# Selective scan on one core: two more products with B on GpSimd, a B tile with an odd offset, and a copied column order in the dt stage

## The chip, the cores and the metric

The kernel runs on one core of a Trainium2 chip. The metric is the device time of one execution in microseconds (us), median of three runs. The engines are named as the profile names them: PE (TensorE matmul) and PEld (its weight loads), DVE (VectorE), ACT (ScalarE), POOL (GpSimd) and SPq (the DMA queue that SyncE feeds).

## The reference, cut to what matters

Layer 0 is a shifted-window attention block on 16 images of 56 x 56 tokens with 192 channels. Layer 1 is a selective scan in four directions (row order, column order, and both reversed) with 16 states for each channel:

```python
xs = _cross_scan(xc)                       # row order, column order, both reversed
x_dbl = jnp.einsum('bkdl,kcd->bkcl', xs, x_proj_weight)
dts, Bs, Cs = jnp.split(x_dbl, [R_RANK, R_RANK + N_STATE], axis=2)
dts = jnp.einsum('bkrl,kdr->bkdl', dts, dt_projs_weight)
dts = jax.nn.softplus(dts + dt_projs_bias[None, :, :, None])
...
dA = jnp.exp(dt_t[..., None] * A)
dBx = (dt_t * x_t)[..., None] * B_t[:, :, None, :]
h = dA * h_prev + dBx
y = jnp.einsum('bkdn,bkn->bkd', h, C_t)
```

## The kernel before

The program has four stages, one after the other: layer 0, the dt stage (`build_prep`), the scan (`build_scan`) and the output. Between stages the data lies in HBM. Each engine has its own written-out order of work and waits on counters (semaphores) of the others. The change touches the two middle stages.

**The dt stage** makes dt, u = dt * x, B and C. It works image by image, in four chunks (`PAIRS`) of 784 positions, and in each chunk on six tiles (`TILES`) of 128 rows: tiles 0 to 2 are the row order (o = 0), tiles 3 to 5 the column order (o = 1). A seventh piece of TensorE's work gives B and C. The columns of an image are read in column order by a view of the tile `xm` whose inner step is one image row, 56 words (224 bytes); that is what `order` returns for o = 1. For each tile TensorE computes the raw value into PSUM (L750 to L754, L759 and L762 for B and C), ACT copies it to `xb` (L780, a ring of four), clamps (L793), takes exp (L801) and log (L809, into PSUM). DVE then does four operations per tile: P, the `scalar_tensor_tensor` of `m_t` and the log (L858), then `quad` of the next tile (L848, whose two inputs are both `e_t` in SBUF), then a minimum (L863) and a maximum that gives dt (L867). The other three operations have one operand in PSUM. POOL multiplies dt by x (L884, `times_x`) and splits B and C into three bf16 parts, one operation in each of the places j = 1 to 4 of a chunk (`split`: L894 cast, L898 subtract, L901 cast, L904 subtract). SP stores dt, u, B and C, and loads the next image.

**The scan** has 256 units (16 images, 16 units each: order, chunk, direction), and a unit has 24 steps of 784 positions: three groups of eight state pairs. In a step ACT computes dA (L1133), DVE or POOL the product of u and B, and DVE the scan itself (L1199). In 17 steps DVE multiplies u by a B that TensorE spread into PSUM (L1054, L1176, `DVE_STEPS`), two steps ahead of the scan (`LEAD`). In the other 7 (`POOL_STEPS`, steps 3, 7, 11, 13, 15, 19, 23) POOL multiplies u by a B tile `bp_u` that a DMA loaded for state pairs 3, 5 and 7 (L1224), into the two-buffer ring `dbp`; it does so seven steps ahead. POOL also multiplies each two steps' states by C (L1235, 12 operations of 1568 columns in a unit), into a ring `pr` that TensorE sums (L1065). DVE's scan of a step waits until POOL has done the product with C of the step six earlier (`RH` = 6 buffers of `hs`):

```python
after(dve, prod_done, n - RH + 1)
```

The tiles `hs`, `dbx` and `dbp` are 786 columns wide with their data in columns 1 to 784 (`data`), so their data begins 4 bytes into a row whose start is a multiple of 8 bytes; `u_u`, `c_u`, `pr` and `bp_u` are 784 wide and begin at column 0. SP loads a unit's tiles when POOL has finished the unit two earlier, so they are used one unit later.

Of the kernel before, what the change touches and what calls it, by code (L numbers as in the profile page):

```python
# [556 lines left out]
POOL_STEPS = (3, 7, 11, 13, 15, 19, 23)  # L557
# [20 lines left out]
def build_prep(nc, io, xn, dts, us, bcs, bps, n_img):  # L578
# [7 lines left out]
    with ExitStack() as ctx:  # L586
# [20 lines left out]
        rem = sb("rem", [128, CT])  # L607
        parts = sb("parts", [128, 2, 3, CT], BF16)
# [6 lines left out]
        u_done = sem("u_done")  # L615
# [8 lines left out]
        def order(tile, o, c, h, n):  # L624

            t0 = CT * c + HT * h
            if o == 0:
                return tile[:, t0:t0 + n]
            return tile.rearrange("p (r w) -> p w r", r=IMG)[:, t0 // IMG:(t0 + n) // IMG, :]
# [92 lines left out]
        @block.tensor  # L722
        def _(pe):
            pe.wait_ge(w_in, 80)
            for k in range(4):
                pe.matmul(ps[:, k, 0:C], xpr_sb[:, k, 0:128], dtw_sb[:, k, :], start=True, stop=True)
            for k in range(4):
                pe.matmul(ps[0:64, k, 512:512 + C], xpr_sb[:, k, 128:C], dtw_sb[:, k, :], start=True, stop=True)
            for k in range(4):
                mm = pe.matmul(ps[64:128, k, 512:512 + C], xpr_sb[:, k, 128:C], dtw_sb[:, k, :], start=True, stop=True)  # L730
            mm.then_inc(w_mm, 1)
            pe.wait_ge(w_done, 1)

            def free(b, k):

                img, j = (0, k - 2) if k >= 2 else (-1, k - 2 + PER_IMG)
                if j % PER < TILES:
                    after(pe, xb_done, TILES * (PAIRS * (b + img) + j // PER) + j % PER + 1)
                else:
                    after(pe, bc_done, PAIRS * (b + img) + j // PER + 1)  # L740

            def body(b, par, last):
                pe.wait_ge(x_in[par], images_in(b, par))
                for k in range(PER_IMG):
                    c, j = k // PER, k % PER
                    free(b, k)
                    if j < TILES:
                        o, m0 = j // 3, 128 * (j % 3)
                        for h in range(2):
                            pe.matmul(bank(k, h), wk[:, o, 0, m0:m0 + 128], order(xm[:, par, 0, :], o, c, h, HT),  # L750
                                      start=True, stop=False)
                        pe.matmul(bank(k, 0), wk[0:64, o, 1, m0:m0 + 128], order(xm[0:64, par, 1, :], o, c, 0, HT),
                                  start=False, stop=True)
                        pe.matmul(bank(k, 1), wk[64:128, o, 2, m0:m0 + 128], order(xm[64:128, par, 2, :], o, c, 1, HT),  # L754
                                  start=False, stop=True).then_inc(raw_full, 1)
                    else:
                        for h in range(2):
                            for o in range(2):
                                pe.matmul(bank(k, h)[64 * o:64 * o + 64, :], wk[:, o, 0, 2 * C:KC],  # L759
                                          order(xm[:, par, 0, :], o, c, h, HT), start=True, stop=False)  # L760
                            for o in range(2):
                                mm = pe.matmul(bank(k, h)[64 * o:64 * o + 64, :], wk[0:64, o, 1, 2 * C:KC],  # L762
                                               order(xm[0:64, par, 1, :], o, c, h, HT), start=False, stop=True)
                        mm.then_inc(raw_full, 1)

            halves(pe, body)
# [62 lines left out]
        def _(dve):  # L829
# [20 lines left out]
            def body(b, par, last):  # L850
                for c in range(PAIRS):
                    g = PAIRS * b + c
                    for j in range(TILES):
                        n, o = TILES * g + j, j // 3
                        l = l_ps(j)
                        dve.wait_ge(l_done, n + 1)
                        dve.wait_ge(m_done, n + 1)
                        nc.vector.scalar_tensor_tensor(l, m_t[:, j % 2], -0.5, l, ALU.mult, ALU.max).then_inc(p_done, 1)  # L858
                        at = step(b, n_of(c, j) + 1, last)
                        if at:  # L860
                            quad(*at)
# [11 lines left out]
        def _(pool):  # L873

            def times_x(b, par, c, j):
# [5 lines left out]
                u = u_o[:, o, k, :]  # L881
                if o:
                    dt, u = (a.rearrange("p (w r) -> p w r", r=IMG) for a in (dt, u))
                nc.gpsimd.tensor_tensor(u, dt, order(xm[:, par, k, :], o, c, 0, CT), ALU.mult).then_inc(u_done, 1)  # L884
# [21 lines left out]
            def body(b, par, last):  # L906
                pool.wait_ge(x_in[par], images_in(b, par))
                for c in range(PAIRS):
                    for j in range(TILES):
# [4 lines left out]
                        elif not (isinstance(b, int) and b == 0):  # L914
                            times_x(b - 1, 1 - par, PAIRS - 1, TILES - 1)
                        if j in (1, 2, 3, 4):
# [8 lines left out]

            halves(pool, body)


def build_scan(nc, io, dts, us, bcs, bps, ysc, n_img):
# [9 lines left out]
    with ExitStack() as ctx:  # L939
# [18 lines left out]
        bp_u = sb("bp_u", [128, 2, len(POOL_PAIRS), CT])  # L958
# [26 lines left out]
        def _(sp):  # L985
# [5 lines left out]
            def load(b, w):  # L991
# [9 lines left out]
                for h in range(2):  # L1001
                    sp.dma_start(bp_u[64 * h:64 * h + 64, d],
# [211 lines left out]
        def _(pool):  # L1214

            def times_b(b, w, i):
# [4 lines left out]
                if not (isinstance(v, int) and v == 0 and i < RG):  # L1221
# [3 lines left out]
                                        bp_u[:, d, POOL_PAIRS.index(s % NPR), :], ALU.mult).then_inc(bp_done, 1)  # L1225

            def body(b, first, last):
                for w in range(WI):
                    v, d = WI * b + w, w % 2
                    pool.wait_ge(u_in[d], in_of(b, w))  # L1230
                    for s in range(0, STEPS, 2):
# [7 lines left out]
                        elif s + 7 - STEPS == POOL_STEPS[0]:  # L1239
                            if w + 1 < WI:  # L1240
                                times_b(b, w + 1, 0)
                            elif not last:
                                times_b(b + 1, 0, 0)

            times_b(0, 0, 0)
            images(pool, body, n_img)
# [302 lines left out]
```

## Time and profile before

| | us |
|---|---|
| median of three runs | 21221.99 (21221.65 to 21222.45) |
| the profiled execution | 21220.53 |
| its span | 21218.7 |
| dt stage, window taken | 4383 to 6290 |
| scan, window taken | 6334 to 20540 |
| DVE busy in the span | 18936.0 |
| POOL busy in the span | 15154.9 |
| TensorE's mean granted clock | 0.788 |

Busy times are those of one profiled execution. A start-to-start distance of two instructions in the timeline is a little shorter than a duration, because the end of one overlaps the start of the next. A granted clock of 1.00 is TensorE's level of 2.4 GHz, 0.50 that of 1.2 GHz.

### The profile page before, as it was taken

Reading aid. Unit: us, or ns where it says so; the run is one execution under the profiler, and the core shown is the slowest. Engines: PE = TensorE matmul, PEld = TensorE weight load, DVE = VectorE, ACT = ScalarE, POOL = GpSimd, SP = SyncE. Lnnn points to the kernel's source line nnn. Section 1 sums busy time; section 2 is a strip of 40 time slices with the busy share of each in tenths; the row PEclk is TensorE's granted clock in tenths of the full one; section 3 lists DMA queues with packets and bytes.
Section 4 is the critical chain, followed back from the end, with each engine's and each line's share of the span. In section 5 each row is a group of like instructions: output and inputs, shape, how many; then the busy total and the mean of one; then the engine's idle time right before and its main releaser. Section 6 shows DMA issues by size and latency. Waiting matters only on the chain. (4 is left out here: it accounts for less than half of the span.)

```text
span 21218.7 us, 290175 instructions
## 1 busy us (share of the span) xinstructions
PE 16258.9 (77%) x83096; PEld 5510.0 (26%) x83096; DVE 18936.0 (89%) x21113; ACT 10243.6 (48%) x19687; POOL 15154.9 (71%) x5780
## 2 busy tenths in 40 slices
PE   8999999999987777777777777777777777777752
PEld 5555555532221111111111111111111111111112
DVE  5555555579989999999999999999999999999986
ACT  4444444467764444444444444444444444444443
POOL 0000000046669999999999999999999999999988
PEclk9999999988987777777777777777777777777765
DMA  0000000056665666666666666666666666666668
GB/s 22 18 18 18 18 18 17 18 174 230 226 214 122 135 126 134 129 131 131 127 135 129 135 127 131 131 131 133 126 135 127 135 129 130 131 128 135 128 142 230
DMA packets 1091858, 2520.55 MB, mean 119 GB/s; under 512 B 247606, under 2 KB 398648, under 8 KB 1075328
## 3 DMA queue, kind: packets, MB, share of 16 engines
q1 hardware_dynamic: 1090688, 2508.11, 52.6%
q14 instruction: 822, 6.73, 0.1%
q8 instruction: 348, 5.70, 0.1%
HBM read 2000.43 MB, written 507.38 MB: 118 GB/s over the span
## 5 line engine op out<-in xcount | busy, mean ns | idle before, releaser
L1235 POOL TENSOR_TENSOR c_pr<-c_hs,c_c_u 128x1568 f32<-128x1568 f32 x3072 | 9929.8, 3236 | 1040.9 <-DVE c_hs L1199 761.9
L1133 ACT ACTIVATE c_psum<-c_dt_u,c_a_neg 128x784 f32<-128x784 f32 x6144 | 5641.8, 918 | 7476.7 <-DVE c_hs L1199 7419.7
L1199 DVE TENSOR_TENSOR_SCAN c_hs<-c_psum,c_dbx 128x785 f32<-128x785 f32 (+1 forms) x4352 | 7606.2, 1770 | 20.9 <-issue 20.9
L1065 PE MATMUL c_psum<-c_pr,c_red 128*64 128x392 f32 x24576 | 7222.4, 707 | 1.3 <-POOL c_pr L1235 1.3
L1054 PE MATMUL c_psum<-c_br_u,c_sel 48*128 48x512 bf16 (+1 forms) x8704 | 2966.6, 433 | 4024.7 <-DVE c_dbx L1176 3925.3
L1176 DVE TENSOR_TENSOR c_dbx<-c_u_u,c_psum 128x784 f32<-128x784 f32 x4352 | 4086.9, 939 | 39.6 <-PE c_psum L1054 39.6
L1224 POOL TENSOR_TENSOR c_dbp<-c_u_u,c_bp_u 128x784 f32<-128x784 f32 x1792 | 3312.4, 1848 | 105.9 <-DVE c_hs L1199 63.7
L1199 DVE TENSOR_TENSOR_SCAN c_hs<-c_psum,c_dbp 128x785 f32<-128x785 f32 (+1 forms) x1792 | 3186.0, 1778 | 0.0
L196 POOL TENSOR_TENSOR a_xpb<-a_x_sb,a_pb_sb 98x768 f32<-98x768 f32 x128 | 231.1, 1806 | 4062.5 <-DVE a_x L285 4048.9
L1065 PEld LDWEIGHTS c_psum<-c_pr,c_red 128*64 128x64 f32 x24576 | 1790.2, 177 | 3403.3 <-issue 3120.7
L1054 PEld LDWEIGHTS c_psum<-c_br_u,c_sel 48*128 48x128 bf16 x8704 | 522.4, 101 | 8208.9 <-DVE c_dbx L1176 7004.6
L884 POOL TENSOR_TENSOR p_u_o<-p_dt_o,p_xm 128x784 f32<-128x784 f32 x384 | 786.7, 2049 | 715.2 <-DVE p_dt_o L867 715.2
L750 PE MATMUL p_psum<-p_xm,p_wk 128*128 128x392 f32 x1536 | 910.2, 722 | 81.9 <-ACT p_xb L780 70.6
L848 DVE SCALAR_TENSOR_TENSOR p_m_t<-p_e_t 128x784 f32<-128x784 f32 x384 | 777.7, 2025 | 15.2 <-ACT p_e_t L801 15.2
L235 DVE TENSOR_REDUCE a_mx<-a_psum 128x6 f32<-128x294 f32 x512 | 234.2, 457 | 617.2 <-PE a_psum L461 617.2
L329 ACT ACTIVATE a_g_sb<-a_psum,a_b_sb 128x392 f32<-128x392 f32 x768 | 408.6, 583 | 519.1 <-PE a_psum L426 519.1
L424 PE MATMUL a_psum<-a_h2T,a_w_sb 128*128 128x392 f32 x1536 | 609.1, 519 | 60.2 <-ACT a_h2T L312 60.2
L436 PE MATMUL a_psum<-a_g_sb,a_w_sb 128*128 128x392 f32 x1536 | 607.8, 518 | 53.6 <-ACT a_g_sb L329 53.6
L285 DVE TENSOR_TENSOR a_x<-a_xpb,a_psum 98x384 f32<-98x384 f32 x256 | 142.0, 555 | 525.1 <-PE a_psum L536 525.1
L1115 ACT ACTIVATE c_dbx<-c_carry 128x1 f32<-128x1 f32 x3264 | 608.5, 186 | 0.0
L780 ACT ACTIVATE p_xb<-p_psum,p_bpos 128x784 f32<-128x784 f32 x384 | 349.6, 910 | 439.9 <-DVE p_dt_o L867 411.0
L1471 PE MATMUL d_psum<-d_id_sb,d_yf 96*112 96x96 f32 x896 | 155.2, 361 | 510.1 <-POOL d_yf L1350 390.9
(119 smaller groups left out, 17276.6 us busy)
## 6 DMA issues: line engine op xcount, KB each, us to landing
c_c_u<-scr_bc SPq DMA_DIRECT2D x512, 1568.0 KB, 28.7
c_dt_u<-scr_dt SPq DMA_DIRECT2D x512, 588.0 KB, 7.3
c_u_u<-scr_u SPq DMA_DIRECT2D x512, 588.0 KB, 10.9
c_bp_u<-scr_bc SPq DMA_DIRECT2D x512, 588.0 KB, 22.1
scr_dt<-p_dt_o SPq DMA_DIRECT2D x384, 392.0 KB, 3.1
scr_u<-p_u_o SPq DMA_DIRECT2D x384, 392.0 KB, 2.4
scr_y<-c_y_sb SPq DMA_DIRECT2D x256, 294.0 KB, 17.7
d_yin<-scr_y SPq DMA_DIRECT2D x32, 2352.0 KB, 14.5
```

Source lines behind the costliest of these rows:

```text
L424: pe.matmul(ps[:, gate(m + f), 0:UT], w1_sb[:, 0, w(f)], h2T[:, 0, :], start=True, stop=False)
L750: pe.matmul(bank(k, h), wk[:, o, 0, m0:m0 + 128], order(xm[:, par, 0, :], o, c, h, HT), start=True, stop=False)
L848: nc.vector.scalar_tensor_tensor(m_t[:, j % 2], e, -2.0, e, ALU.add, ALU.mult).then_inc(m_done, 1)
L884: nc.gpsimd.tensor_tensor(u, dt, order(xm[:, par, k, :], o, c, 0, CT), ALU.mult).then_inc(u_done, 1)
L1054: mm = pe.matmul(b_ps[:, n0:n1], sel[:, s % NPR, :], br_u[:, d, n0:n1], start=True, stop=True)
L1065: mm = pe.matmul(Y(3 * w + q)[64 * h:64 * h + 64, :], red[:], pr[:, s % RP, HT * h:HT * h + HT], start=(p == 0 and opens(w)), stop=(p == N ...
L1115: nc.scalar.activation(end, carry[:, d, s:s + 1], ACT.Copy)
L1133: nc.scalar.activation(dA(s)[:, data], dt_u[:, d, s // NPR, :], ACT.Exp, scale=a_neg[:, k, s:s + 1]).then_inc(exp_done, 1)
L1176: nc.vector.tensor_tensor(dbx[:, (MULS * w + i) % RB, data], u_u[:, d, s // NPR, :], b_ps, ALU.mult).then_inc(mul_done, 1)
L1199: nc.vector.tensor_tensor_scan(hs[:, s % RH, way], dA(s)[:, way], added, 0.0, ALU.mult, ALU.add).then_inc(scan_done, 1)
L1224: nc.gpsimd.tensor_tensor(dbp[:, (len(POOL_STEPS) * w + i) % RG, data], u_u[:, d, s // NPR, :], bp_u[:, d, POOL_PAIRS.index(s % NPR), :], ...
L1235: nc.gpsimd.tensor_tensor(pr[:, s % RP:s % RP + 2, :], hs[:, s % RH:s % RH + 2, data], c_u[:, d, s % NPR:s % NPR + 2, :], ALU.mult).then_i ...
```

## The change

In the scan POOL takes steps 5 and 21 as well: nine products with B instead of seven, DVE fifteen instead of seventeen. The tile `bp_u` becomes 786 columns wide, with its data in columns 1 to 784. POOL's product for the second place of the next unit is now issued at the end of a unit too.

In the dt stage POOL copies the column-order view of a chunk to a new tile `xt`, contiguous, one chunk ahead (`turn`, three copies in a chunk in the places j = 0, 1 and 3, behind `times_x` and ahead of `split`). TensorE's matmuls and POOL's `times_x` of the column order read `xt`. Ahead of the first column-order tile of a chunk TensorE waits for the chunk's copies. On DVE `quad` of the next tile stands ahead of P instead of behind it.

```diff
-POOL_STEPS = (3, 7, 11, 13, 15, 19, 23)
+POOL_STEPS = (3, 5, 7, 11, 13, 15, 19, 21, 23)
...
+        xt = sb("xt", [128, 2, 3, CT])
...
-        def order(tile, o, c, h, n):
-
-            t0 = CT * c + HT * h
+        def order(rows, par, k, o, c, h, n):
+
             if o == 0:
-                return tile[:, t0:t0 + n]
-            return tile.rearrange("p (r w) -> p w r", r=IMG)[:, t0 // IMG:(t0 + n) // IMG, :]
+                return xm[rows, par, k, CT * c + HT * h:CT * c + HT * h + n]
+            return xt[rows, c % 2, k, HT * h:HT * h + n]
...
+                    if j == TILES // 2:
+                        pe.wait_ge(turned, 3 * (PAIRS * b + c) + 3)
...
+                        at = step(b, n_of(c, j) + 1, last)
+                        if at:
+                            quad(*at)
                         dve.wait_ge(l_done, n + 1)
                         dve.wait_ge(m_done, n + 1)
                         nc.vector.scalar_tensor_tensor(l, m_t[:, j % 2], -0.5, l, ALU.mult, ALU.max).then_inc(p_done, 1)
-                        at = step(b, n_of(c, j) + 1, last)
-                        if at:
-                            quad(*at)
...
-                u = u_o[:, o, k, :]
-                if o:
-                    dt, u = (a.rearrange("p (w r) -> p w r", r=IMG) for a in (dt, u))
-                nc.gpsimd.tensor_tensor(u, dt, order(xm[:, par, k, :], o, c, 0, CT), ALU.mult).then_inc(u_done, 1)
+                nc.gpsimd.tensor_tensor(u_o[:, o, k, :], dt, order(slice(0, 128), par, k, o, c, 0, CT),
+                                        ALU.mult).then_inc(u_done, 1)
+
+            def turn(b, par, c, k):
+
+                g = PAIRS * b + c
+                if k == 0:
+                    if c == 0:
+                        hold(pool, x_in[par], images_in(b, par), fence)
+                    if not (isinstance(g, int) and g < 2):
+                        hold(pool, u_done, TILES * (g - 1), fence)
+                        hold(pool, raw_full, PER * (g - 1), fence)
+                cols = xm[:, par, k, :].rearrange("p (r w) -> p w r", r=IMG)[:, CT * c // IMG:CT * (c + 1) // IMG, :]
+                nc.gpsimd.tensor_copy(xt[:, c % 2, k, :].rearrange("p (w r) -> p w r", r=IMG), cols).then_inc(turned, 1)
...
+                        if j in (0, 1, 3):
+                            if c + 1 < PAIRS:
+                                turn(b, par, c + 1, (0, 1, 3).index(j))
+                            elif not last:
+                                turn(b + 1, 1 - par, 0, (0, 1, 3).index(j))
...
+            for k in range(3):
+                turn(0, 0, 0, k)
...
-        bp_u = sb("bp_u", [128, 2, len(POOL_PAIRS), CT])
+        bp_u = sb("bp_u", [128, 2, len(POOL_PAIRS), CT + 2])
...
-                    sp.dma_start(bp_u[64 * h:64 * h + 64, d],
+                    sp.dma_start(bp_u[64 * h:64 * h + 64, d, :, data],
...
-                                        bp_u[:, d, POOL_PAIRS.index(s % NPR), :], ALU.mult).then_inc(bp_done, 1)
+                                        bp_u[:, d, POOL_PAIRS.index(s % NPR), data], ALU.mult).then_inc(bp_done, 1)
...
-                        elif s + 7 - STEPS == POOL_STEPS[0]:
+                        elif s + 7 - STEPS in POOL_STEPS:
+                            i = POOL_STEPS.index(s + 7 - STEPS)
                             if w + 1 < WI:
-                                times_b(b, w + 1, 0)
+                                times_b(b, w + 1, i)
                             elif not last:
-                                times_b(b + 1, 0, 0)
+                                times_b(b + 1, 0, i)
 
             times_b(0, 0, 0)
+            times_b(0, 0, 1)
```

## Rows read from the trace of the kernel before

**Rows 1.** By window: us, busy (PE, PEld, DVE, ACT, POOL), clock, DMA.

```profile
4383.00:6290.00 1907.00, 1786.31 (x4090) 471.70 (x4088) 1806.79 (x1536) 1359.43 (x1600) 1280.47 (x639) 0.90 0.66 223
6334.00:20540.00 14206.00, 10241.70 (x34048) 2462.22 (x34048) 14175.67 (x10496) 6720.68 (x13568) 13097.21 (x4864) 0.72 0.63 130
```

**Rows 2.** The page's costliest groups, those of the scan.

```profile
L1235 POOL TENSOR_TENSOR c_pr<-c_hs,c_c_u 128x1568 f32<-128x1568 f32 x3072 | 9929.8, 3236 | 1040.9 <-DVE c_hs L1199 761.9
...
L1199 DVE TENSOR_TENSOR_SCAN c_hs<-c_psum,c_dbx 128x785 f32<-128x785 f32 (+1 forms) x4352 | 7606.2, 1770 | 20.9 <-issue 20.9
...
L1176 DVE TENSOR_TENSOR c_dbx<-c_u_u,c_psum 128x784 f32<-128x784 f32 x4352 | 4086.9, 939 | 39.6 <-PE c_psum L1054 39.6
L1224 POOL TENSOR_TENSOR c_dbp<-c_u_u,c_bp_u 128x784 f32<-128x784 f32 x1792 | 3312.4, 1848 | 105.9 <-DVE c_hs L1199 63.7
```

**Rows 3.** Timeline of VectorE in the scan: start, us, operation.

```profile
12004.18 1.78 DVE L1199 TENSOR_TENSOR_SCAN c_hs<-c_psum,c_dbx 128x785 f32<-128x785 f32 x1
...
12006.75 3.46 DVE L1199 TENSOR_TENSOR_SCAN c_hs<-c_psum,c_dbx 128x785 f32<-128x785 f32 x2
12010.13 0.94 DVE L1176 TENSOR_TENSOR c_dbx<-c_u_u,c_psum 128x784 f32<-128x784 f32 x1
```

**Rows 4.** Timeline of GpSimd in the scan.

```profile
12022.23 1.84 POOL L1224 TENSOR_TENSOR c_dbp<-c_u_u,c_bp_u 128x784 f32<-128x784 f32 x1 [0.24 <-DVE c_hs L1199]
12024.02 6.43 POOL L1235 TENSOR_TENSOR c_pr<-c_hs,c_c_u 128x1568 f32<-128x1568 f32 x2
12030.41 1.84 POOL L1224 TENSOR_TENSOR c_dbp<-c_u_u,c_bp_u 128x784 f32<-128x784 f32 x1
```

**Rows 5.** Timeline of the DMA queue in the scan.

```profile
12053.77 1.38 SPq L997 DMA_DIRECT2D c_dt_u<-scr_dt  x2
...
12060.15 0.74 SPq L1004 DMA_DIRECT2D c_c_u<-scr_bc  x1
...
12109.14 1.38 SPq L997 DMA_DIRECT2D c_dt_u<-scr_dt  x2
```

**Rows 6.** Landing of the last load: DMA issues, KB each, us to landing.

```profile
c_c_u<-scr_bc SPq DMA_DIRECT2D x512, 1568.0 KB, 28.7
```

**Rows 7.** GpSimd's groups by shape, whole span.

```profile
L1350 POOL TENSOR_TENSOR d_yf<-d_yin 96x3136 f32<-96x3136 f32 x32 | 267.3, 8355 | 39.5 <-DVE d_yin L1383 39.5
```

**Rows 8.** The dt stage by line: times run, shortest, median, longest in ns.

```profile
L884 POOL TENSOR_TENSOR p_u_o<-p_dt_o,p_xm x384: 1840/2048/2272, 4394.7 to 6284.8; 128x784 f32<-128x784 f32 x192
...
L894 POOL CAST p_parts<-p_bc_o x64: 836/1585/1600, 4431.6 to 6286.9; 128x784 bf16<-128x784 f32 x64
...
L898 POOL TENSOR_TENSOR p_rem<-p_bc_o,p_parts x64: 1665/2404/2426, 4436.3 to 6287.8; 128x784 f32<-128x784 f32 x64
...
L848 DVE SCALAR_TENSOR_TENSOR p_m_t<-p_e_t x384: 968/2056/2429, 4388.4 to 6277.5; 128x784 f32<-128x784 f32 x192
```

**Rows 9.** Timeline of the dt stage.

```profile
5200.97 0.97 DVE L863 TENSOR_TENSOR p_psum<-p_psum,p_e_t 128x784 f32<-128x784 f32 x1
5201.98 0.97 DVE L867 TENSOR_TENSOR p_dt_o<-p_xb,p_psum 128x784 f32<-128x784 f32 x1
...
5202.86 0.97 DVE L858 SCALAR_TENSOR_TENSOR p_psum<-p_m_t,p_psum 128x784 f32<-128x784 f32 x1
5203.03 1.85 POOL L884 TENSOR_TENSOR p_u_o<-p_dt_o,p_xm 128x784 f32<-128x784 f32 x1 [1.28 <-DVE p_dt_o L867]
...
5203.74 1.97 DVE L848 SCALAR_TENSOR_TENSOR p_m_t<-p_e_t 128x784 f32<-128x784 f32 x1
...
5204.84 2.40 POOL L898 TENSOR_TENSOR p_rem<-p_bc_o,p_parts 128x784 f32<-128x784 f32 x1
...
5205.56 1.58 PE L750 MATMUL p_psum<-p_xm,p_wk 128*128 128x392 f32 x4
...
5213.27 3.13 PE L750 MATMUL p_psum<-p_xm,p_wk 128*128 128x392 f32 x4 [0.52 <-ACT p_xb L780]
```

**Rows 10.** Busy time in one tile of the copied order, columns as in rows 1.

```profile
5213.20:5218.30 5.10, 4.75 (x8) 1.02 (x8) 5.07 (x5) 3.47 (x6) 4.67 (x3) 1.00 0.41 161
```

More of the change, by code:

```diff
@@ L614, in build_prep @@
         m_done, p_done, q_done, dt_done = sem("m_done"), sem("p_done"), sem("q_done"), sem("dt_done")
-        u_done = sem("u_done")
+        u_done, turned = sem("u_done"), sem("turned")
         hi_done, rem_done, mid_done, low_done = sem("hi_done"), sem("rem_done"), sem("mid_done"), sem("low_done")
@@ L749, in body @@
                         for h in range(2):
-                            pe.matmul(bank(k, h), wk[:, o, 0, m0:m0 + 128], order(xm[:, par, 0, :], o, c, h, HT),
+                            pe.matmul(bank(k, h), wk[:, o, 0, m0:m0 + 128], order(slice(0, 128), par, 0, o, c, h, HT),
                                       start=True, stop=False)
-                        pe.matmul(bank(k, 0), wk[0:64, o, 1, m0:m0 + 128], order(xm[0:64, par, 1, :], o, c, 0, HT),
+                        pe.matmul(bank(k, 0), wk[0:64, o, 1, m0:m0 + 128], order(slice(0, 64), par, 1, o, c, 0, HT),
                                   start=False, stop=True)
-                        pe.matmul(bank(k, 1), wk[64:128, o, 2, m0:m0 + 128], order(xm[64:128, par, 2, :], o, c, 1, HT),
+                        pe.matmul(bank(k, 1), wk[64:128, o, 2, m0:m0 + 128], order(slice(64, 128), par, 2, o, c, 1, HT),
                                   start=False, stop=True).then_inc(raw_full, 1)
@@ L759, in body @@
                                 pe.matmul(bank(k, h)[64 * o:64 * o + 64, :], wk[:, o, 0, 2 * C:KC],
-                                          order(xm[:, par, 0, :], o, c, h, HT), start=True, stop=False)
+                                          order(slice(0, 128), par, 0, o, c, h, HT), start=True, stop=False)
                             for o in range(2):
                                 mm = pe.matmul(bank(k, h)[64 * o:64 * o + 64, :], wk[0:64, o, 1, 2 * C:KC],
-                                               order(xm[0:64, par, 1, :], o, c, h, HT), start=False, stop=True)
+                                               order(slice(0, 64), par, 1, o, c, h, HT), start=False, stop=True)
                         mm.then_inc(raw_full, 1)
```

## The prediction

> **What bounds the kernel now.** I read the busy times by stage first. In the scan's window DVE is busy 14176 of 14206 us and POOL 13097; in the dt stage DVE 1807 of 1907 and PE 1786 [rows 1]. DVE sets the pace of the scan alone: a scan followed by a product takes 2.57 us (12004.18 to 12006.75), two scans without a product between them 3.38, so 1.69 each [rows 3]. Seventeen of the one and seven of the other give 17 x 2.57 + 7 x 1.69 = 55.5 us; from one unit's first load to the next unit's is 55.37 [rows 5]. POOL is close behind: two products with C take 6.39 us from start to start (3.195 each), a product with B 1.79 [rows 4], so a unit has 12 x 3.195 + 7 x 1.80 = 50.9 us of POOL's work and 4.4 us of rest.
>
> The dt stage spreads 384 tiles over 1890 us (first to last start of POOL's u product, 383 intervals, 4.94 us each), so 29.6 us for a chunk of six [rows 8]. The slow piece is `quad` (L848): it runs in 0.97 us at best and takes 2.06 in the median. The timeline shows what holds it: POOL's u product starts at 5203.03, `quad` at 5203.74, and `quad` ends at 5205.71, 0.87 us after POOL's next start at 5204.84 [rows 9]. The reverse holds too: that POOL subtract takes 2.40 us, 1.665 at best, and the cast 1.585, 0.836 at best [rows 8, 9]. So `quad` and a POOL operation exclude each other, and the one that waits gets in when the other ends, even if POOL has more queued. DVE's other three operations keep 0.97 beside POOL; only `quad` has two inputs in SBUF.
>
> **The scan's change.** Two products leave DVE. Each is worth 2.57 - 1.69 = 0.88 us, since a scan then follows a scan. 2 x 0.88 x 256 units = 450 us, and the unit becomes 55.37 - 1.76 = 53.61 us, if DVE still sets the pace.
>
> POOL gets nine products with B. At their present price it needs 12 x 3.195 + 9 x 1.80 = 54.54 us, more than DVE's 53.61, and POOL would be the bound. So all hangs on what the odd offset of `bp_u` does. Before shows no product with B in the new form. The nearest row is the product with C: 1568 columns in 3236 ns, 2.06 ns a column, against 1848 ns for 784, 2.36 [rows 2]. Part of this is a fixed cost. POOL's two operations with one strided input give it: 3136 columns in 8355 ns [rows 7] and 784 in some 2250 (the longest is 2272 [rows 8]), so 2.60 ns a column and 0.21 us fixed. With 0.21 fixed, the product with C runs at 1.93 ns a column and the one with B at 2.09. Only a fixed cost of 0.46 us would make them equal, and then the whole-tile cast would have 0.38 us for 784 columns, four times the rate of the product. What differs is the placing: C's product reads `hs` from an odd word and `c_u` from an even one; B's reads both from even ones, and the contiguous u product of the dt stage, both even too, takes 1840 ns at best [rows 8]. An odd output alone does not help, as B's has one. The padded tile gives B's product C's placing, so I take 0.21 + 784 x 1.93 ns = 1.725 us (0.12 less), 1.68 from start to start. POOL then needs 38.34 + 9 x 1.68 = 53.5 us, just under DVE's. The bounds: 1.62 with no fixed cost, 1.85 if the offset does nothing, 2.25, the strided row, if it harms.
>
> Can two engines this close run without stopping each other? I laid out eight steps by the code's waits. DVE's eight steps take 17.9 us, POOL's four products with C and three with B 17.8. POOL's product for step 7 stands behind the product with C of steps 0 and 1 but reuses the buffer of step 3's scan; POOL then starts some 1 us later than it could, keeps that lag, and meets no further wait. DVE needs that product with C only at step 6, 5 us later. So neither stops the other. The loads: the last is issued 6.4 us after the first [rows 5] and lands 28.7 us on [rows 6], 35 of a unit's 53; they are needed at step 20, at 45 us. The number and size of transfers do not change. If they were slower by the odd offset, ten us cover it. ACT waits on DVE's scan throughout (two scans in a row stand in rows 3 already) and is not reached.
>
> **The dt stage's change.** Three pieces.
>
> PE: a tile of the row order has its first four matmuls in 1.58 us, one of the column order in 3.13 [rows 9], at a granted clock of 1.00, so 2.4 GHz, in that very tile [rows 10]. It is the strided read, not the clock. Read from `xt` they are all fast. PE's chunk is 1786 / 64 = 27.9 us busy [rows 1], a third of it row order and two thirds column order; with the latter halved it is 18.6, no bound, and even at the scan's granted clock (0.72 [rows 1]) 18.6 / 0.72 = 25.8 us. POOL's u product of the column order falls from 2.25 to 1.85.
>
> DVE: its tile costs 0.88 between operations that don't depend on each other (max to P, P to `quad`), 1.01 between min and max that do [rows 9]. In the new order P to min also depends: 0.88 + 0.88 + 1.01 + 1.01 = 3.78 us if `quad` never waits. `quad` now follows the max directly and takes the port before the u product that waits for that max; POOL starts 0.9 us later, under DVE's three other operations. DVE then waits only for what POOL still has queued.
>
> POOL: three copies more in a chunk, each with one strided input. No such row exists. Below, the contiguous cast at its best, 0.84; above, the strided two-input product, 2.25. I take half of the contiguous product for its contiguous read, and the rest of the strided one for the strided: 2.25 - 0.85 = 1.4 us.
>
> A chunk laid out by hand, from the port's rule: after a max, `quad` holds the port 0.87, the u product 1.81, then the extras. Where a copy follows (three places) `quad` waits 0.87 + 1.81 + 1.4 - 3.78 = 0.3 us; where a subtract ends last (two places, behind a cast that came late) 0.87 + 0.80 + 1.81 + 1.62 - 3.78 = 1.3 us. Chunk: 6 x 3.78 + 3 x 0.3 + 2 x 1.3 = 26.2 us. Saved: (29.6 - 26.2) x 64 = 218 us. With a copy of 0.84 the chunk is some 24.7 (313 us saved), with 2.25 it is 28.8 (51 saved). The three copies ahead of the loop run under the first tiles of the row order.
>
> The Trainium skill's GPSIMD Engine Reference, section Performance pitfalls for Q7 kernels, prices reads with a step above 8 bytes at about 2.9 cycles an element. At 1.2 GHz that is an estimate of 1.9 us for a copy, a chunk of 27.7 and 122 us saved, 96 less than my sum; its contiguous 1.9 cycles are more than the cast shows here (0.836 us for 784, 1.3 cycles).
>
> **Sum.** 21220.5 of the profiled execution (1.5 us below the median) - 450 - 218 = 20553 us.
>
> **Rivals.**
> POOL becomes the bound of the scan. The offset does nothing, POOL needs 54.54 us, the scan saves (55.37 - 54.54) x 256 = 212 instead of 450: 21220.5 - 212 - 218 = 20790. For it: the product with C also differs by its length and its two-row shape, and the fixed cost is from operations of another form. Against: that fixed cost would have to be double.
> The same page, section Instruction dispatch, gives about 2.5 cycles an element as the floor of a two-input operation and says nothing of offsets; by it the price stays and this rival is the result. The row of the product with C (2.06 ns, 2.5 cycles) fits that floor, the one with B (2.8 cycles) leaves room above it.
>
> The port takes the dt stage's gain. If POOL's longer queue keeps `quad` out for more than one operation, DVE waits a copy and a cast or the u product as well and a chunk stays near 29.6: 21220.5 - 450 = 20770. Against it stands the subtract that let `quad` in [rows 9].
>
> Slower: the odd offset harms the second input. Priced as the strided row, 2.25 us (2.21 from start to start), a unit takes 38.34 + 9 x 2.21 = 58.2 us, 2.86 more than now, + 732 - 218: 21735. It decides from a product of 1.99 us start to start, since 9 x 1.99 + 38.34 = 56.2 eats the dt stage's 0.85 us a unit. Against: `hs` is read at an odd word at the better rate.
>
> **How the numbers follow.** Forecast 0.60, POOL as bound 0.27, the port 0.08, the slower one 0.04, nothing gained at all 0.01. A measurement of this kernel tells 0.2%, some 42 us, from no change. All but the last two are faster: faster 0.95, same 0.01, slower 0.04. The forecast's own range is 20450 (copies at 0.84) to 20720 (2.25). POOL as bound reaches from 20695 to 20957; I go up to 20840 and leave its tail and the slower case out.
>
> **What would show it.** Scan: L1224 at 1.72 us, DVE without idle, load to load 53.6 us. At 1.85 POOL has no idle, DVE waits for L1235 or L1224, and load to load is 54.5. dt stage: `quad` near 0.97 to 2.3 with waits behind L904 and L898; PE's four matmuls 1.58 us in all tiles; a new copy of 1.4 us; u product 1.85, shown longer where it waits for `quad`. The prediction fails most easily on B's product and on the copy.

## The result, and the profile after

The changed kernel takes 20603.72 us (median of four runs, 20602.78 to 20604.99) against 21222.22; the ratio is 0.9708, 95% interval 0.9692 to 0.9725. The forecast was 20553 us, 51 us too low; the range of 20450 to 20840 holds it.

Busy times of the dt stage and of the scan after the change, columns as in [rows 1]:

```profile
4383.00:6120.00 1737.00, 1338.75 (x4096) 482.57 (x4094) 1642.29 (x1540) 1359.57 (x1600) 1589.69 (x832) 0.86 0.72 245
6157.00:19925.00 13768.00, 9529.81 (x33024) 2403.81 (x33024) 13725.95 (x9984) 6717.75 (x13568) 13665.17 (x5376) 0.74 0.65 134
```

The first line answers to the dt stage's of before: the stage is shorter and PE's work in it fell from 1786 to 1339 us. The second is the scan: DVE is busy 13726 of 13768 us and POOL 13665, so both engines are now full.

The costliest groups of the scan, from the page:

```profile
L1254 POOL TENSOR_TENSOR c_pr<-c_hs,c_c_u 128x1568 f32<-128x1568 f32 x3072 | 9908.8, 3236 | 13.4 <-DVE c_hs L1218 12.9
...
L1218 DVE TENSOR_TENSOR_SCAN c_hs<-c_psum,c_dbx 128x785 f32<-128x785 f32 (+1 forms) x3840 | 6737.2, 1770 | 20.7 <-issue 20.7
...
L1218 DVE TENSOR_TENSOR_SCAN c_hs<-c_psum,c_dbp 128x785 f32<-128x785 f32 (+1 forms) x2304 | 4104.9, 1782 | 11.4 <-ACT c_psum L1152 11.4
L1243 POOL TENSOR_TENSOR c_dbp<-c_u_u,c_bp_u 128x784 f32<-128x784 f32 x2304 | 3943.0, 1711 | 127.8 <-DVE c_hs L1218 76.3
L1195 DVE TENSOR_TENSOR c_dbx<-c_u_u,c_psum 128x784 f32<-128x784 f32 x3840 | 3621.8, 943 | 39.9 <-PE c_psum L1073 39.9
```

They answer to [rows 2]. DVE does 3840 products instead of 4352, at nearly the same duration (943 ns, 939 before). POOL does 2304 products with B instead of 1792, at 1711 ns instead of 1848. POOL's rest ahead of the products with C fell from 1041 to 13 us.

From the first to the last scan the stage took 14193 us before and 13755 now, 55.44 and 53.73 us a unit: 438 us saved. From the first to the last u product the dt stage took 1890 us before and 1710 now, 29.6 and 26.8 us a chunk: 180 us saved. Together they are the 618 us of the result; the other stages kept their time.

The mean of 1711 ns hides what matters. The timeline of GpSimd in the scan:

```profile
12036.79 3.24 POOL L1254 TENSOR_TENSOR c_pr<-c_hs,c_c_u 128x1568 f32<-128x1568 f32 x1
12039.99 1.58 POOL L1243 TENSOR_TENSOR c_dbp<-c_u_u,c_bp_u 128x784 f32<-128x784 f32 x1
12041.52 3.24 POOL L1254 TENSOR_TENSOR c_pr<-c_hs,c_c_u 128x1568 f32<-128x1568 f32 x1
12044.72 1.85 POOL L1243 TENSOR_TENSOR c_dbp<-c_u_u,c_bp_u 128x784 f32<-128x784 f32 x1
12046.52 6.42 POOL L1254 TENSOR_TENSOR c_pr<-c_hs,c_c_u 128x1568 f32<-128x1568 f32 x2
```

The product with B takes 1.58 us or 1.85 us, nothing between. Going through all 2304 in order, and naming them by the tile row that they read (six rows: two directions times three pairs), each row has one duration (median of 384 products each):

| row of `bp_u` (a word is 4 bytes) | 0 | 1 | 2 | 3 | 4 | 5 |
|---|---|---|---|---|---|---|
| begins, in words modulo four | 1 | 3 | 1 | 3 | 1 | 3 |
| us | 1.575 | 1.850 | 1.573 | 1.846 | 1.575 | 1.840 |

Every tile starts at a multiple of four words in these kernels, so the places can be counted from the tile's start. A row is 786 words, two more than a multiple of four, so the rows alternate. Half of the products gained 0.27 us, half gained nothing.

In the dt stage, lines with times run and shortest, median and longest in ns:

```profile
L883 POOL TENSOR_TENSOR p_u_o<-p_dt_o,p_xm x192: 1835/2582/2615, 4397.4 to 6096.9; 128x784 f32<-128x784 f32 x192
...
L896 POOL COPY p_xt<-p_xm x192: 1621/1644/1697, 4382.4 to 6074.7; 128x784 f32<-128x784 f32 x192
...
L850 DVE SCALAR_TENSOR_TENSOR p_m_t<-p_e_t x384: 968/1328/2165, 4391.7 to 6100.6; 128x784 f32<-128x784 f32 x192
...
L752 PE MATMUL p_psum<-p_xt,p_wk x768: 492/493/1023, 4391.2 to 6088.3; 128*128 128x392 f32 x192
```

And of the timeline, the first four matmuls of a column-order tile:

```profile
5165.57 1.58 PE L752 MATMUL p_psum<-p_xt,p_wk 128*128 128x392 f32 x4
```

`quad` (L850) has a median of 1.33 us instead of the 2.06 of [rows 8]. The u product (L883) is shown at 2.58, since it now starts behind `quad` and its wait for the port is in its span; 1.84 is its own time. A copy takes 1.64 us. Four of TensorE's matmuls of the column order in a row now take 1.58 us, as those of the row order did; before they took 3.13 [rows 9].

The same stage in order of time:

```profile
5178.45 1.64 POOL L896 COPY p_xt<-p_xm 128x784 f32<-128x784 f32 x1
5178.73 0.97 DVE L869 TENSOR_TENSOR p_dt_o<-p_xb,p_psum 128x784 f32<-128x784 f32 x1
...
5179.62 1.32 DVE L850 SCALAR_TENSOR_TENSOR p_m_t<-p_e_t 128x784 f32<-128x784 f32 x1
...
5180.05 1.58 POOL L906 CAST p_parts<-p_bc_o 128x784 bf16<-128x784 f32 x1
...
5180.86 0.97 DVE L863 SCALAR_TENSOR_TENSOR p_psum<-p_m_t,p_psum 128x784 f32<-128x784 f32 x1
```

The copy (L896) starts at 5178.45, and DVE's maximum (L869) runs beside it at its usual 0.97. `quad` starts at 5179.62 and ends at 5180.94, 0.85 us after the copy's end (5180.09); the cast behind the copy, 0.83 us at its best, then takes 1.58. This is the exclusion of [rows 9], with a copy as the one that goes first: `quad` loses 0.35 us here, where it lost 1.0 in [rows 9]. It holds throughout: 307 of the 384 `quad`s take over 1.05 us while a POOL operation ends inside them, and each of these ends 0.83 to 0.85 us after that operation's end.

### The profile page after: what moved, and what is told of

It reads as the page before. It is cut to its first block and busy times, and to the rows that moved or that the text cites. A ratio compares the mean times of both kernels' runs of the same rounds, so it can differ in the third digit from the quotient of the medians.

```text
span 20602.3 us, 287674 instructions
## 1 busy us (share of the span) xinstructions
PE 15096.4 (73%) x82072; PEld 5460.7 (27%) x82072; DVE 18321.8 (89%) x20601; ACT 10241.1 (50%) x19687; POOL 16030.5 (78%) x6484
## 5 line engine op out<-in xcount | busy, mean ns | idle before, releaser
L1254 POOL TENSOR_TENSOR c_pr<-c_hs,c_c_u 128x1568 f32<-128x1568 f32 x3072 | 9908.8, 3236 | 13.4 <-DVE c_hs L1218 12.9
L1084 PE MATMUL c_psum<-c_pr,c_red 128*64 128x392 f32 x24576 | 6829.8, 679 | 5.9 <-POOL c_pr L1254 5.9
L1218 DVE TENSOR_TENSOR_SCAN c_hs<-c_psum,c_dbx 128x785 f32<-128x785 f32 (+1 forms) x3840 | 6737.2, 1770 | 20.7 <-issue 20.7
L1073 PE MATMUL c_psum<-c_br_u,c_sel 48*128 48x512 bf16 (+1 forms) x7680 | 2596.8, 430 | 4293.5 <-DVE c_dbx L1195 4191.0
L1218 DVE TENSOR_TENSOR_SCAN c_hs<-c_psum,c_dbp 128x785 f32<-128x785 f32 (+1 forms) x2304 | 4104.9, 1782 | 11.4 <-ACT c_psum L1152 11.4
L1243 POOL TENSOR_TENSOR c_dbp<-c_u_u,c_bp_u 128x784 f32<-128x784 f32 x2304 | 3943.0, 1711 | 127.8 <-DVE c_hs L1218 76.3
L1195 DVE TENSOR_TENSOR c_dbx<-c_u_u,c_psum 128x784 f32<-128x784 f32 x3840 | 3621.8, 943 | 39.9 <-PE c_psum L1073 39.9
L850 DVE SCALAR_TENSOR_TENSOR p_m_t<-p_e_t 128x784 f32<-128x784 f32 x384 | 579.4, 1509 | 46.3 <-ACT p_e_t L803 26.7
L752 PE MATMUL p_psum<-p_xt,p_wk 128*128 128x392 f32 x768 | 364.1, 604 | 270.7 <-ACT p_xb L782 270.2
L1134 ACT ACTIVATE c_dbx<-c_carry 128x1 f32<-128x1 f32 x2880 | 537.0, 186 | 0.0
L883 POOL TENSOR_TENSOR p_u_o<-p_dt_o,p_xt 128x784 f32<-128x784 f32 x192 | 442.7, 2306 | 85.1 <-DVE p_dt_o L869 83.7
```

Of the source, the lines that this page charges most:

```text
L850: nc.vector.scalar_tensor_tensor(m_t[:, j % 2], e, -2.0, e, ALU.add, ALU.mult).then_inc(m_done, 1)
L883: nc.gpsimd.tensor_tensor(u_o[:, o, k, :], dt, order(slice(0, 128), par, k, o, c, 0, CT), ALU.mult).then_inc(u_done, 1)
L1073: mm = pe.matmul(b_ps[:, n0:n1], sel[:, s % NPR, :], br_u[:, d, n0:n1], start=True, stop=True)
L1084: mm = pe.matmul(Y(3 * w + q)[64 * h:64 * h + 64, :], red[:], pr[:, s % RP, HT * h:HT * h + HT], start=(p == 0 and opens(w)), stop=(p == N ...
L1134: nc.scalar.activation(end, carry[:, d, s:s + 1], ACT.Copy)
L1195: nc.vector.tensor_tensor(dbx[:, (MULS * w + i) % RB, data], u_u[:, d, s // NPR, :], b_ps, ALU.mult).then_inc(mul_done, 1)
```

## The experiments

### Nine products from an unpadded tile

```diff
-        bp_u = sb("bp_u", [128, 2, len(POOL_PAIRS), CT + 2])
+        bp_u = sb("bp_u", [128, 2, len(POOL_PAIRS), CT])
```

The load and the product use columns 0 to 783 accordingly.

> The changed kernel, with the B tile 784 columns wide again, data from the first column. In the changed kernel the product with B shows two durations: 1.57 us for rows 0, 2 and 4 of the tile (of six, two directions times three pairs) and 1.85 us for rows 1, 3 and 5; the tile is 786 words wide, so even rows begin 1 word and odd rows 3 words behind a multiple of four words. Theory (the placing of the second input sets the rate): all nine products take 1.85 us, GpSimd needs 12 x 3.195 + 9 x 1.80 = 54.54 us a unit against 53.73 now, and becomes the bound: 20604 + 0.81 x 256 = 20811 us. Rival (the two durations come from what else runs at that moment, not from the tile's place): two durations stay, time 20604.

Measured: 20826.29 us, ratio to before 0.9813 (0.9797 to 0.9829). The product with B over the whole run, and the scan's window:

```profile
L1243 POOL TENSOR_TENSOR c_dbp<-c_u_u,c_bp_u x2304: 1825/1855/2007, 6156.8 to 20134.6; 128x784 f32<-128x784 f32 x192
```

```profile
6157.00:20140.00 13983.00, 9539.74 (x33002) 2395.61 (x33002) 13763.85 (x9984) 6715.86 (x13567) 13964.59 (x5375) 0.74 0.64 132
```

All six rows have medians of 1.85 to 1.86 us, POOL is busy 13965 of 13983 us and DVE only 13764. A unit is 54.59 us, where the sum of POOL's operations gave 54.54. This is the prediction's first rival, made to happen: without the offset POOL is the bound, and the offset is worth 223 us here.

### A probe of all places

```diff
-        bp_u = sb("bp_u", [128, 2, len(POOL_PAIRS), CT + 2])
+        bp_u = sb("bp_u", [128, 2, len(POOL_PAIRS), CT + 1])
...
-        hs = sb("hs", [128, RH, CT + 2])
+        hs = sb("hs", [128, RH, CT + 3])
```

The data of `bp_u` begins at column 0, so that its row r begins r words on.

> A probe in the changed kernel: the B tile is 785 words wide with data from the first column, so its six rows begin 0, 1, 2, 3, 4 and 5 words behind the start; the state tile hs is 787 wide, so its six rows begin 1, 0, 3, 2, 1, 0 words (modulo 4) behind a multiple of four. Theory (place modulo four words): the product with B takes 1.57 us at rows 1 and 5, 1.85 at 0, 3 and 4; row 2 is not known from what has run, 1.57 or 1.85. The product with C, two rows in one operation, took 3.235 with rows at 1 and 3, as one fast and one slow half would; now it must show at least two durations over its three row pairs (3.23 for a fast and a slow half, some 3.5 for two slow ones, some 2.95 for two fast ones). Rival (every second row is fast, whatever its place): B rows 0, 2 and 4 at 1.57 and C at 3.235 throughout. GpSimd gets slower in the mean: some 20700 to 20850 us.

Measured: 20804.41 us, one run. GpSimd's timeline:

```profile
12010.02 1.88 POOL L1243 TENSOR_TENSOR c_dbp<-c_u_u,c_bp_u 128x784 f32<-128x784 f32 x1
12011.82 3.54 POOL L1254 TENSOR_TENSOR c_pr<-c_hs,c_c_u 128x1568 f32<-128x1568 f32 x1
12015.29 1.89 POOL L1243 TENSOR_TENSOR c_dbp<-c_u_u,c_bp_u 128x784 f32<-128x784 f32 x1
12017.11 2.99 POOL L1254 TENSOR_TENSOR c_pr<-c_hs,c_c_u 128x1568 f32<-128x1568 f32 x1
12020.03 1.60 POOL L1243 TENSOR_TENSOR c_dbp<-c_u_u,c_bp_u 128x784 f32<-128x784 f32 x1
```

The product with C (L1254) now has two durations as well, 3.54 and 2.99 here. By rows, medians over the run:

| operation | first input begins at | second input at | second behind first, modulo four words | us |
|---|---|---|---|---|
| B, rows 0 and 4 | 0 | 0 | 0 | 1.85, 1.87 |
| B, rows 1 and 5 | 0 | 1 | 1 | 1.57 |
| B, row 2 | 0 | 2 | 2 | 1.58 |
| B, row 3 | 0 | 3 | 3 | 1.85 |
| C, `hs` rows 0 and 1, or 4 and 5 | 1 and 0 | 0 | 3 and 0 | 3.51 |
| C, `hs` rows 2 and 3 | 3 and 2 | 0 | 1 and 2 | 2.96 |

One rule fits all lines: fast when the second input begins 1 or 2 words behind the first, modulo four words, slow at 0 or 3. Offset 2 is even and fast, offset 3 is odd and slow, so "odd" was the wrong word. The rival, every second row whatever its place, is out: row 1 was slow before and is fast here. In all these products one of the two inputs begins at a multiple of four words; what happens when both begin off it was not tried, so "behind the first" is shown for these pairs alone.

### Wider rows, both ways round

Both kernels make `bp_u` and `hs` 788 words wide, so that all their rows begin alike. In the first `hs` begins one word behind a multiple of four, in the second three:

```diff
-        bp_u = sb("bp_u", [128, 2, len(POOL_PAIRS), CT + 2])
+        bp_u = sb("bp_u", [128, 2, len(POOL_PAIRS), CT + 4])
...
-        hs = sb("hs", [128, RH, CT + 2])
+        hs = sb("hs", [128, RH, CT + 4])
```

> The changed kernel with the B tile and the state tile hs 788 columns wide, data from the second column in both, so every row begins one word behind a multiple of four. From the probe: a two-input product on GpSimd is fast when its second input begins 1 or 2 words behind the first (modulo four words), slow at 0 or 3. Theory: the product with B (u at 0, B at 1) takes 1.57 us in all rows; the product with C (hs at 1, C at 0, so 3 behind) has two slow halves, 3.50. GpSimd needs 12 x 3.47 + 9 x 1.53 = 55.4 us a unit, and the time is 20604 + (55.4 - 53.73) x 256 = some 21030 us. Rival (an odd word in either input is enough): both fast, 2.96 for C, time 20604 or a little less.

Measured: 21087.46 us, ratio 0.9925 (0.9893 to 0.9956), over 400 us slower than the changed kernel. The profiled execution took 21045, with a unit of 55.44 us where the expectation had 55.4; why the other seven took some 40 us more is not known.

```profile
L1243 POOL TENSOR_TENSOR c_dbp<-c_u_u,c_bp_u x2304: 1561/1577/2005, 6155.3 to 20350.4; 128x784 f32<-128x784 f32 x192
...
L1254 POOL TENSOR_TENSOR c_pr<-c_hs,c_c_u x3072: 3475/3526/3963, 6163.5 to 20358.9; 128x1568 f32<-128x1568 f32 x192
```

The second kernel has this in place of the last line:

```diff
+        hs = sb("hs", [128, RH, CT + 4])[:, :, 2:CT + 4]
```

> As the run with rows of 788, but hs begins at the fourth column (3 words behind a multiple of four), so C is 1 word behind it. Theory: product with C 2.96, with B 1.57; GpSimd needs 12 x 2.92 + 9 x 1.53 = 48.8 us a unit and no longer matters; VectorE's 53.6 us set the time, 20604 less the 0.1 us a unit that VectorE now loses: 20575 to 20604 us. Rival (VectorE loses more to GpSimd than its idle time shows): clearly below 20570 us.

Measured: 20588.45 us, ratio 0.968 (0.9606 to 0.9753).

```profile
L1243 POOL TENSOR_TENSOR c_dbp<-c_u_u,c_bp_u x2304: 1562/1575/1617, 6155.4 to 19894.4; 128x784 f32<-128x784 f32 x192
...
L1254 POOL TENSOR_TENSOR c_pr<-c_hs,c_c_u x3072: 2949/2962/2980, 6163.7 to 19902.1; 128x1568 f32<-128x1568 f32 x192
```

Two kernels that differ by two columns' shift of one tile: the product with C takes 3.53 us in one and 2.96 in the other, with no overlap between the ranges. The rule holds whichever of the two inputs is the displaced one. Twice 1.575 less 2.962 leaves 0.19 us as the fixed cost of one operation, close to the 0.21 of the prediction.

In the second kernel POOL has time to spare; its waits show it (us in total, times, longest):

```profile
POOL c_dbp L1243 <- DVE c_hs L1218: 915.5, 766, 1.2
```

The changed kernel had 75 us there. A unit is 53.68 us, VectorE's own work, and 15 us of the time were gained: that is what the near tie cost the changed kernel. It did not cost it as a wait of VectorE for GpSimd; no such wait is in the changed kernel's list. These are:

```profile
ACT c_y_sb L1142 <- DMA scr_y<-c_y_sb: 74.9, 29, 3.8
...
DVE c_hs L1218 <- ACT c_psum L1152: 11.4, 17, 1.2
```

ScalarE waits for the store of y, and VectorE 11.4 us for ScalarE's exp behind it. With GpSimd faster the first wait is 42.4 us and the second is gone. In the code SyncE issues that store behind a unit's loads, which wait for GpSimd's products, so a late GpSimd makes the store late; this link is read from the code and not tested by itself. The wait for the store is taken away below, with eleven products.

### The dt stage alone, and its two halves

Only the dt stage's change, with the scan of before:

> Only the change of the dt stage; the scan is as before (seven products, B tile 784 wide). If the two parts add up: dt stage 177 us shorter as in the changed kernel, so 21222 - 177 = 21045 us, and the product with B at 1.85. Rival (the parts interact, since the scan's first loads or the order of buffers profit): differs from 21045 by over 40 us.

Measured: 21040.29 us, ratio 0.9914 (0.9898 to 0.9931); the chunk is 26.79 us, the unit 55.44. The parts add up within 5 us.

Only the order on DVE (`quad` ahead of P), in the kernel before:

> The kernel before, with quad ahead of P on VectorE and nothing else. Theory (TensorE's strided reads are the next bound): quad no longer waits for the u product, but TensorE needs 27.9 us of work for a chunk of 29.6, so the chunk falls to 28 us at best and the copies are needed for the rest: 21222 - (29.6 - 28.0) x 64 = 21120 us, and TensorE idles hardly at all. Rival (VectorE and the port alone set the pace): without the copies GpSimd has less on the port, the chunk is 22.7 + 2 x 1.3 + 0.4 for the longer u product = 25.7 us, and the time 20970 us.

Measured: 21123.04 us, ratio 0.9954 (0.9937 to 0.997). The dt stage, and `quad`:

```profile
4383.00:6191.00 1808.00, 1759.51 (x4088) 435.12 (x4087) 1489.58 (x1536) 1349.85 (x1600) 1301.05 (x639) 0.99 0.69 235
```

```profile
L848 DVE SCALAR_TENSOR_TENSOR p_m_t<-p_e_t x384: 966/968/2421, 4388.1 to 6178.7; 128x784 f32<-128x784 f32 x192
```

`quad` has a median of 0.97 us, most of its waits are gone, and yet the chunk is 28.07 us: PE is busy 1760 of 1808 us at a granted clock of 0.99, in effect the level of 2.4 GHz. The strided reads of the column order are the bound, as the first theory had it.

Only the copies, with `quad` behind P as before:

> The changed kernel with quad behind P again, so that of the dt stage's change only the copied column order is left. Theory (VectorE and the port are the bound, as the prediction has it): quad waits for the whole u product again, 4.66 us for a tile as the row-order tiles had, and a copy with a cast behind it delays the next u product by some 0.5 us in two places: a chunk of 28.0 + 0.6 = 28.6 us against 26.8, and 20604 + 1.8 x 64 = 20719 us. Rival (TensorE's faster reads alone were most of the gain): 20604 to 20640 us.

Measured: 20742.39 us, ratio 0.9774 (0.9758 to 0.979), the chunk 28.96 us.

```profile
L850 DVE SCALAR_TENSOR_TENSOR p_m_t<-p_e_t x384: 968/1968/2272, 4390.3 to 6238.0; 128x784 f32<-128x784 f32 x192
```

`quad` waits for the u product again, 1.97 in the median. Each half alone gives little, 1.5 us of a chunk for the order and 0.65 for the copies; together they give 2.8. Each takes away a bound that hides the other's gain.

### The copies on ScalarE

`turn` moves from POOL to ACT as `nc.scalar.activation(..., ACT.Copy)`, in the places j = 2, 3 and 4; POOL waits for `turned` ahead of the first column-order product.

> The changed kernel with the three copies of a chunk on ScalarE instead of GpSimd (places j = 2, 3 and 4 of a chunk). Theory (a copy costs by the wait for the port that it puts ahead of quad): quad's three waits behind the copies, 3 x 0.54 us, go; a chunk falls from 26.8 to 25.2 us, 20604 - 1.6 x 64 = 20500 us. Rival (ScalarE, with 21.2 us of work in a chunk and some 1 us for each copy, delays the exp and log that VectorE waits for): no gain or a loss, 20604 or more.

Measured: 20600.77 us, ratio 0.9708 (0.9692 to 0.9724), the same as the changed kernel. The dt stage; DVE's wait for the exp; the copies:

```profile
4383.00:6110.00 1727.00, 1326.95 (x4093) 470.67 (x4092) 1552.01 (x1540) 1632.90 (x1791) 1267.55 (x640) 0.87 0.73 246
```

```profile
DVE p_m_t L870 <- ACT p_e_t L803: 116.2, 105, 15.9
```

```profile
L823 ACT ACTIVATE p_xt<-p_xm x192: 1641/1665/1715, 4380.5 to 6063.3; 128x784 f32<-128x784 f32 x192
```

The rival was right. The port is relieved (DVE is busy 1552 instead of 1642 us), but a copy takes ACT 1.67 us, not 1, and ACT is busy 1633 of 1727 us; DVE waits 116 us for the exp, 27 in the changed kernel. In a chunk the waits inside `quad` fell by 1.5 us and those for the exp rose by 1.4. A copy takes nearly the same on both engines (1.64 and 1.67 us). Its length alone does not make it so: ACT's exp and clamp of 784 contiguous columns take 0.94 us in the same run.

### x one word off in the dt stage

```diff
-        xm = sb("xm", [128, 2, 3, L])
+        xm = sb("xm", [128, 2, 3, L + 4])[:, :, :, 1:L + 1]
...
-        xt = sb("xt", [128, 2, 3, CT])
+        xt = sb("xt", [128, 2, 3, CT + 4])[:, :, :, 1:CT + 1]
```

> The changed kernel, with x and its copied column order in the dt stage one word behind a multiple of four (both tiles four columns wider). Theory: the u product falls from 1.85 to 1.57 us, quad's waits by 0.28 us in five places of a chunk, 1.4 x 64 = 90 us: 20515 us. Rival 1 (waits are set by the subtracts and copies alone): 20604 us. Rival 2 (TensorE reads x at an odd word more slowly): the matmuls of the dt stage get longer and the gain is lost.

Measured: 20529.64 us, ratio 0.9652 (0.9579 to 0.9725), 74 us below the changed kernel; the chunk is 25.64 us.

```profile
L883 POOL TENSOR_TENSOR p_u_o<-p_dt_o,p_xm x192: 1563/2299/2330, 4396.7 to 6022.7; 128x784 f32<-128x784 f32 x192
...
L850 DVE SCALAR_TENSOR_TENSOR p_m_t<-p_e_t x384: 968/1060/2269, 4390.9 to 6026.4; 128x784 f32<-128x784 f32 x192
```

The u product is 1.56 us at its best instead of 1.84, and `quad` has a median of 1.06 us; its waits fell by 1.25 us a chunk, a little less than five times 0.28. The rule of the scan holds in another stage.

### Eleven products on GpSimd

With both products fast, POOL has room. `POOL_PAIRS` becomes (1, 3, 5, 7) and POOL takes all odd steps but step 1; DVE keeps thirteen.

> The kernel with the fast placings, and eleven products with B on GpSimd (all odd steps but step 1; the B tile holds four state pairs), thirteen on VectorE. Theory (work of the two engines is all that counts): VectorE 53.61 - 2 x 0.88 = 51.9 us a unit, GpSimd 12 x 2.92 + 11 x 1.53 = 51.9: 20604 - 1.8 x 256 = 20140 us at best. Rival (at a tie the two engines stop each other: a product with B two steps after the last reuses a ring buffer that is free only when the scan is there): some 0.5 to 1 us a unit more, 20270 to 20400 us.

Measured: 20285.21 us, ratio 0.9537 (0.9465 to 0.9609), a unit of 52.47 us where the work alone gives 51.9. The time lies in the range that the rival named, but not for the rival's reason. Waits of its scan:

```profile
ACT c_y_sb L1142 <- DMA scr_y<-c_y_sb: 216.3, 30, 8.0
...
DVE c_hs L1218 <- ACT c_psum L1152: 121.8, 26, 5.3
...
DVE c_hs L1218 <- POOL c_pr L1254: 17.8, 5, 3.6
```

POOL is not it: DVE waits 18 us for it. ACT waits 216 us for the store of y before it may write the y tile again, its exp stands behind that, and DVE waits 122 us for the exp. With x one word off as well:

> The kernel with the fast placings and eleven products with B on GpSimd, and with x one word off in the dt stage too. If the two gains add up: 20285 - 74 = 20211 us.

Measured: 20215.11 us, ratio 0.9525 (0.9509 to 0.9541). They add up. Then a fifth y tile, for the unit that opens an order right after the one that closed the same chunk:

```diff
-        y_sb = sb("y_sb", [128, NCHK, 3, HT])
+        y_sb = sb("y_sb", [128, NCHK + 1, 3, HT])
...
+        def place(o, cc):
+
+            return NCHK if o and cc == 0 else cc
```

> The kernel with eleven products and x one word off, and a fifth tile for the scan's results y, so that the unit that opens an order no longer writes the tile that the unit just before it closed. In the run with eleven products a unit took 52.47 us where 53.68 - 2 x 0.88 = 51.92 were expected; ScalarE waited 216 us for the transfer that stores y, and VectorE 122 us for ScalarE's next exp. Theory (that wait is the difference): a unit falls to some 51.95 us, the time to 20215 - 0.53 x 256 = 20080 us. Rival (the tie between VectorE and GpSimd costs the half microsecond, and would show as waits for GpSimd once ScalarE's is gone): 20180 to 20215 us.

Measured: 20070.0 us, ratio 0.9457 (0.9441 to 0.9472), a unit of 51.92 us. What is left of VectorE's and GpSimd's waits in the scan:

```profile
DVE c_hs L1222 <- issue: 21.4, 13, 2.1
POOL c_dbp L1247 <- DVE c_hs L1222: 13.5, 13, 1.1
```

No wait of ACT for the store and none of DVE for ACT or POOL remains in the list of waits. The unit is what DVE's work adds up to. This version beats both kernels: 1152 us below the kernel before, 534 below the changed one.

## Why the prediction was right, and where it was off

**What bounds the scan.** Right. Two products fewer are worth 0.88 us each: 55.44 less 1.76 is 53.68, the unit of the kernel with fast placings, and eleven products give 51.92. Forecast 450 us, measured 438. "Neither stops the other" held: VectorE has no listed wait for GpSimd. The 12 us missing are nearly all the 11.4 us that VectorE waited for ScalarE, behind the store of y; they came back (15 us) when POOL got faster.

**The product with B.** The size was right, 1.725 forecast and 1.711 measured, and with it the step on which all hung; in part this was luck. The mechanism was half right. The prediction reasoned that C's product is faster by its placing and that the padded tile would give B the same. It does. But C's 2.06 ns a column was itself a mean of a fast and a slow half, since `hs` rows alternate like the padded rows of `bp_u`. I read it as one rate and called the cause an odd word. An odd first input and an odd second one are not the same thing either: one word off is slow for `hs`, the first input, and fast for `bp_u`, the second. The means agree only because both tiles have rows of 786 words, which put half of the operations on the fast side. The probe put the rule in its place. Had `bp_u` been 788 words wide, the same argument would have missed by 0.15 us an operation, and the lower bound that the prediction gave for this product, 1.62 us, is above what half of the products took.

**POOL as the bound** (0.27) is what happens without the offset: 54.59 us a unit against 54.54 forecast. The Trainium skill's GPSIMD Engine Reference, section Instruction dispatch, gives some 2.5 cycles an element as the floor for two inputs, by which this rival would have come out. The runs differ: (1.575 - 0.19) us for 784 columns is an estimated 2.1 cycles at the 1.2 GHz that the Trainium skill's GPSIMD Engine Reference, section Specifications, gives for the engine.

**The slower rival** did not come for the product with B: no place of `bp_u` costs more than the 1.85 us of before. That a place can harm was right all the same: with all rows of `hs` one word behind, the product with C takes 3.53 us instead of 3.24.

**The dt stage.** Forecast 218 us, measured 180; this is 38 of the 51 us by which the forecast was low. The copy was mis-sized: 1.4 us assumed, 1.64 measured. By the prediction's own rule each of three waits grows by 0.24 us, so the chunk is 26.2 + 0.72 = 26.9 us, against 26.8 measured. That this comes out is chance, as `quad`'s group on the profile's page and DVE's other waits in the stage show:

```profile
L850 DVE SCALAR_TENSOR_TENSOR p_m_t<-p_e_t 128x784 f32<-128x784 f32 x384 | 579.4, 1509 | 46.3 <-ACT p_e_t L803 26.7
```

```profile
DVE p_m_t L850 <- issue: 18.9, 6, 3.2
DVE p_dt_o L869 <- DVE p_psum L865: 11.5, 56, 0.2
```

At a mean of 1.509 us the waits inside `quad` are (1.509 - 0.967) x 6 = 3.25 us a chunk, not the 3.5 of the layout and still less the 4.2 that it gives with the measured copy. By places, medians: 0.57, 0.35 and 0.33 us behind a copy, where the rule gives 0.54 with the measured copy, 1.18 twice behind a subtract instead of 1.3, and none in the sixth. DVE's own 22.7 us (6 x 3.78) were right. The remaining 0.8 us of the 26.8 are rests of DVE that the layout put at nothing, ahead of `quad` above all, in part for the exp. So two terms were too low, the copy and the rests, the layout's waits were too long for such a copy, and the errors cancel. What the 18.9 us ahead of `quad` that the profile gives no releaser for are stays open.

The lower end of the range rested on a chunk of 24.7 us with a copy of 0.84. The terms as printed give 22.7 + 2 x 1.3 = 25.3 us there, 276 us saved instead of 313; the range would begin some 40 us higher and hold the result as well. The Trainium skill's GPSIMD Engine Reference, section Performance pitfalls for Q7 kernels, led to an estimate of 1.9 us for the copy, as far off on the other side.

**The three pieces.** That TensorE's strided read must go was shown by the order alone (28.07 us, PE full); that the order must go with it, by the copies alone (28.96 us). **The port as rival** was wrong: none of the changed kernel's 384 `quad`s spans the end of more than one POOL operation. That POOL's durations enter DVE's time through this exclusion was shown by the x placing: a u product 0.28 us shorter gave 1.15 us of a chunk, with nothing changed on DVE, against 1.4 for five places times 0.28.

**Loads and queues.** The loads stayed covered, as said. The store of y, which the prediction had not looked at, did not quite: it cost 11 us at nine products already, and at eleven it came to the front.

## What to carry to other kernels

Before moving work to GpSimd, sort its durations by the buffer row they read: a two-valued duration says that the place of the operands matters, and two columns of padding may be worth as much as the move itself (223 us here, against 217 for the move without them). A mean over such a group is not a rate to extrapolate from. Where two bounds lie close together, take both away before judging either: alone each looks like a small gain. After each step ask which transfer's slack has just been used up.

## What the runs showed of the hardware that was not expected

GpSimd's contiguous float32 products on two SBUF inputs have two rates. For 784 columns 1.57 us when the second input begins 1 or 2 words behind the first, modulo four words, and 1.85 us at 0 or 3; for 1568 columns 2.96 and 3.51 to 3.53. In each pair one input began at a multiple of four words. The output's place made no difference: products into both rows of `dbp`, which begin 1 and 3 words on, took the same. Whether larger steps than four words matter was not tried.

TensorE read a float32 moving operand with a step of 224 bytes at half the rate of a contiguous one, four matmuls of 392 columns in 3.13 us against 1.58, both at a granted clock of 1.00; an odd first word cost it nothing (492 ns in the run with x one word off).
